# Experts and attention in one program, the first step reordered, the padding zeroed later, one-hot products a slot later

## What is computed

```python
xn = _layernorm(x)                                   # (4, 1024, 512): 4096 tokens of 512
# attention of xn, four batches of 1024 tokens, causal
x_norm = layernorm(xn) * gamma + beta
q, k, v = x_norm @ qkv[:, :512], x_norm @ qkv[:, 512:1024], x_norm @ qkv[:, 1024:]
s = softmax(causal(q @ k.T / sqrt(512))) @ v @ o_proj + xn
# mixture of eight experts of hidden width 352, two for each token, and two shared ones
gates = softmax(xn @ router_w.T); the two largest, divided by their sum
routed = sum over the two of gate * (silu(xn @ wg[e]) * (xn @ wu[e])) @ wd[e]
shared = (silu(xn @ sg) * (xn @ su)) @ sd            # width 704 = 2 x 352
out = x + s * silu(routed + shared)
```

## Time and profile before

| | us |
|---|---|
| median of three runs (lowest, highest) | 1158.92 (1158.82, 1160.46) |
| the profiled execution's own time | 1158.34 |
| its span, first to last instruction | 1156.6 |
| TensorE busy | 1132.1 (98%) |
| VectorE, ScalarE, GpSimd busy | 570.5, 473.5, 423.4 |
| mean granted clock of TensorE | 0.998 |

### The profile page before, as it was taken

One profiled execution on the slowest core, in us unless ns is written; L12 is line 12 of the kernel. 1 busy time (PEld: TensorE's weight loads), 2 busy tenths in 40 slices (PEclk: granted clock), 3 DMA queues, 4 the chain that ended last, 5 costly groups with the idle time before them and its releaser, 6 DMA issues. The chain is left out here.

```text
span 1156.6 us, 21228 instructions
## 1 busy us (share of the span) xinstructions
PE 1132.1 (98%) x6598; PEld 627.3 (54%) x6599; DVE 570.5 (49%) x1236; ACT 473.5 (41%) x859; POOL 423.4 (37%) x656
## 2 busy tenths in 40 slices
PE   8899999999999999999999999998999999999997
PEld 5555555555555555555555555554454444444454
DVE  6866667677468322211221122111377467467467
ACT  5544444444332223322332233224645545654643
POOL 1363333332200122222222222212764764764663
PEclk9999999999999999999999999999999999999999
DMA  9889999989633589989898878776767668766355
GB/s 288 232 190 219 232 233 236 202 220 231 158 71 77 117 170 209 207 198 209 193 203 191 185 173 182 179 169 163 152 163 186 157 160 184 166 161 182 114 150 126
DMA packets 365004, 209.31 MB, mean 181 GB/s; under 512 B 304309, under 2 KB 314817, under 8 KB 364937
## 3 DMA queue, kind: packets, MB, share of 16 engines
q1 hardware_dynamic: 354104, 172.76, 64.7%
q0 software_dynamic: 10800, 35.69, 12.2%
q10 hardware_dynamic: 32, 0.02, 0.0%
HBM read 89.44 MB, written 46.01 MB: 117 GB/s over the span
## 5 line engine op out<-in xcount | busy, mean ns | idle before, releaser
L708 PE MATMUL pair<-arena 128*128 (+2 forms) x3240 | 506.2, 313 | 0.2 <-issue 0.2
L708 PEld LDWEIGHTS pair<-arena 128*128 128x128 f16 x3240 | 316.1, 98 | 182.6 <-issue 0.9
L1629 DVE SCALAR_TENSOR_TENSOR arena<-pair,slot_unit,arena 128x352 f32<-128x352 f32 x71 | 41.4, 583 | 268.8 <-ACT arena L1519 220.3
L715 PE MATMUL bank<-arena 128*128 x639 | 149.3, 379 | 1.3 <-DMA arena<-arena 1.3
L1519 ACT ACTIVATE arena<-pair,slot_unit 128x352 f32<-128x352 f32 x71 | 39.4, 555 | 205.5 <-PE pair L708 172.1
L1238 POOL COPY arena<-token_of 128x1 uint32 (+1 forms) x71 | 13.0, 183 | 271.3 <-issue 103.3
L715 PEld LDWEIGHTS bank<-arena 128*128 128x128 f16 x639 | 62.5, 98 | 67.7 <-issue 1.8
L1910 PE MATMUL pair<-arena 128*128 128x512 f16 (+3 forms) x576 | 97.5, 326 | 0.6 <-ACT arena L1979 0.6
L1923 PE MATMUL bank<-arena 128*128 128x512 f16 x411 | 93.4, 379 | 0.0
L1240 POOL DMA_INDIRECT arena<-xn_rows,arena x71 | 71.4, 1005 | 55.7 <-POOL arena L1238 54.1
L1895 PE MATMUL bank<-arena 128*128 128x512 f16 x384 | 86.0, 379 | 1.6 <-PEq L1058 1.6
(11 more groups left out here) (205 smaller groups left out, 1356.4 us busy)
## 6 DMA issues: line engine op xcount, KB each, us to landing
slot_rows<-arena SPq DMA_DIRECT2D x71, 256.0 KB
arena<-in_L_attn_x_dram SPq DMA_DIRECT2D x64, 256.0 KB, 3.6
xn_rows<-arena SPq DMA_DIRECT2D x32, 260.0 KB, 2.5
shared_rows<-arena SPq DMA_DIRECT2D x32, 256.0 KB
arena<-shared_rows SPq DMA_DIRECT2D x32, 256.0 KB
out_dram<-arena SPq DMA_DIRECT2D x31, 256.0 KB, 2.8
arena<-in_L_ffn_wg_dram SPq DMA_DIRECT2D x32, 176.0 KB, 3.1
arena<-in_L_ffn_wu_dram SPq DMA_DIRECT2D x32, 176.0 KB, 3.4
```

The lines of the kernel that those rows point to most:

```text
L708: last = pe.matmul(bank[:, 0:width], xt[:, a, c, :], weights(c, b, col, width), start=(c == 0 and i == 0), stop=(c == KC - 1 and i == 2))
L715: last = pe.matmul(bank[:, :], ht[:, a, c, :], weights(c, b), start=(start and c == 0 and i == 0), stop=(stop and c == HC - 1 and i == 2))
L1629: v.scalar_tensor_tensor(sbuf[u], u_banks[u][:, 0:H], slot_unit[u][:, 1:2], sbuf[u], ALU.mult, ALU.mult).then_inc(slot_h_ready, 1)
```

## The change

It has four parts.

1. The second block is gone. The attention's programs become functions that are called at the end of each engine's list in the one block. TensorE's first projection (`first_project`) stands between the down products of the last two slot tiles, and the order of the first two PSUM banks is swapped so that it has a free one. In place of the barrier each engine waits for what it needs: SP and GpSimd for all slot rows to be stored (`slots_stored`), ScalarE for the last slot product, and three of the first batch's projections for copies out of their banks.
2. In SP's queue the stores of tiles 0 and 1 and the first load of `w_down` go behind the first turn of h; on ScalarE and VectorE the second unit's h in the first step goes ahead of tile 2's x and of three of the four splits.
3. GpSimd's memset of the padding goes from between tiles 3 and 4 to behind the last tile.
4. One-hot table 6 is made half a step earlier, and products 1 and 4 are multiplied half a step later.

```diff
@@ fold_programs, sync
                 turn_x16(sp, 1)
-                for t in range(2):
-                    store_x16(sp, t)
@@ routing, hot_products_in
                 elif at == 9:
                     one_hot(dve, 5)
-                elif at == 10:
                     one_hot(dve, 6)
+                elif at == 10:
                     one_hot(dve, 7)
...
-                return {7: (0, 1), 8: (2,), 9: (3, 4), 10: (5,), 11: (6, 7)}.get(at, ())
+                return {7: (0,), 8: (1, 2), 9: (3,), 10: (4, 5), 11: (6, 7)}.get(at, ())
@@ expert_stages, sync
                     for i in in_chunks(0)[:1]:
                         load_in(i)
-                    for s in range(NT):
+                    load_x(3)
+                    turn_h(0)
+                    for t in range(2):
+                        store_x16(sp, t)
+                    load_down(0)
+                    for i in [*in_chunks(0)[1:], *in_chunks(1)[:1]]:
+                        load_in(i)
+                    for s in range(1, NT):
...
                     for j in range(T - 3, T):
                         store_slot_y(j)
+                    attn_sync(sp)
@@ expert_stages, gpsimd
                     x_low(pool, 3)
-                    if HR < P:
-                        pool.wait_ge(shared_lo, len(splits))
-                        pool.memset(w_down[HR:P, :, HC - 1], 0.0).then_inc(down_padded, 1)
-                        pool.wait_ge(down_padded, 1)
...
                     put(pool.memset(segment[:, :, 0:1], 0.0))
+                    pool.wait_ge(consts, n[0])
+                    if HR < P:
+                        pool.wait_ge(shared_lo, len(splits))
+                        pool.memset(w_down[HR:P, :, HC - 1], 0.0).then_inc(down_padded, 1)
+                        pool.wait_ge(down_padded, 1)
@@ expert_stages, tensor
                     slot_down(T - 2, 1, (T - 2) // 2)
+                    first_project(pe)
                     slot_down(T - 1, 0, (T - 1) // 2)
+                    attn_tensor(pe)
@@ first_step, scalar
                         split_hi(act, IN_SPLITS)
-                        split_hi(act, IN_SPLITS + 1)
+                        h_high(1, 1)
                         for t in normal_in(0):
                             x_high(t)
-                        h_high(1, 1)
-                        split_hi(act, IN_SPLITS + 2)
-                        split_hi(act, IN_SPLITS + 3)
+                        for n in range(1, 4):
+                            split_hi(act, IN_SPLITS + n)
@@ first_step, vector
+                        hidden(1, 1)
                         for t in normal_in(0):
                             normalise(dve, t)
-                        hidden(1, 1)
                         split_lo(dve, IN_SPLITS)
-                        split_lo(dve, IN_SPLITS + 1)
                         h_low(1, 1)
-                        split_lo(dve, IN_SPLITS + 2)
-                        split_lo(dve, IN_SPLITS + 3)
+                        for n in range(1, 4):
+                            split_lo(dve, IN_SPLITS + n)
@@ stage4
-            proj_banks = banks[6], banks[7], banks[0], banks[1], banks[2], banks[3]
+            proj_banks = banks[7], banks[6], banks[0], banks[1], banks[2], banks[3]
...
+            def slots_stored(eng):
+                eng.wait_ge(slot_y_done, SLOT_TILES)
+                eng.wait_ge(slot_rows_stored[0], (SLOT_TILES + 1) // 2 * 16)
+                eng.wait_ge(slot_rows_stored[1], SLOT_TILES // 2 * 16)
...
-            with nc.Block() as block:
...
+                slots_stored(sp)
...
+            def gpsimd(pool):
+                slots_stored(pool)
                     pool.memset(causal, 0.0).then_inc(causal_zeroed, 1)
...
+            def project(pe, b, g_):
...
+                if b == 0 and g_ == 1:
+                    pe.wait_ge(slot_y_ready, SLOT_TILES - 1)
+                elif b == 0 and g_ == 2:
+                    pe.wait_ge(slot_h_ready, SLOT_TILES)
+                elif b == 0 and g_ == PG - 2:
+                    pe.wait_ge(slot_y_ready, SLOT_TILES)
...
+            def first_project(pe):
+                pe.wait_ge(fold_loaded, QT * 16)
+                project(pe, 0, 0)
...
+                act.wait_ge(slot_y_done, SLOT_TILES)
```

712 lines of the change are left out of this document (353 added, 359 removed).

## The result

The changed kernel takes 1151.79 us, the median of six runs (1149.63 to 1154.26), beside 1157.89 us for the kernel before; the ratio is 0.9942, 95% interval 0.9930 to 0.9955. Run again later beside the experiments it took 1154.46 us (five runs) against 1159.18, ratio 0.9963 (0.9949 to 0.9977). So it saves 4.7 to 6.1 us. The first median is the forecast of 1151.8 us, but partly because the kernel before was 1.03 us faster in this comparison than in the three runs that the forecast started from: the forecast gain of 7.1 us lies above both measured gains, inside the interval of the first (5.2 to 8.1) and outside that of the second (2.7 to 5.9). The profiled execution took 1151.93 us, with a span of 1150.2. Two executions were slow ones, 1323.11 us in run 10 and 6861.79 us of the kernel before beside run 12; they count in the medians shown and not in the ratios.

The account below looks back on a forecast made before the run. TensorE, busy 98% of the span, was taken as the bound; gains 3.24, 0.94 and 3.25 less a 0.3 loss took 7.1 from 1158.34, giving 1151.2, plus 0.58 for the median: 1151.8 us, range 1149.8 to 1156.0.

Parts of the forecast that it names:

- The seam: Between experts and attention: the first projection fills TensorE's waits, the second starts at 795.00 instead of 798.24; gain 3.24 us.
- Rival 3, the attention restarts late: First attention batch: later gathers delay ScalarE's exp and TensorE waits; up to 3.9 us lost, 1155.7 us; chance 8%.
- The one-hot products: Around 360 us: VectorE bounds the stage, its last table is ready 0.94 us earlier; gain 0.94, between 0 and 3.18.
- The padding: Moving GpSimd's 6.92 us memset from 58.70 removes TensorE's waits at 78.88, 96.76 and 103.46; gain 3.25, between 0 and 3.7.
- The first step: Expert half's start: wait at 48.88 grows to 3.1, that at 55.76 nearly goes; loss 0.3, between gain 1.9 and loss 2.6.
- The order of the two engines: First step: GpSimd's low part of x starts ahead of VectorE's weight split; if VectorE comes first, TensorE starts 1.6 us later.
- the sum itself: Over the whole kernel: the four terms added, -3.24 - 0.94 + 0.3 - 3.25 = -7.1 us.
- a microsecond won ahead of it stays won: Behind the seam TensorE does not wait until far into the last batch, so time won earlier is kept in full.
- The clock: First step: a fall to 1.2 GHz for 3.4 us after TensorE idles, costing 1.7 us; part of rival 1.
- rival 1: First step: the store lands slowest, costing 2.3 us delay and 1.7 us of lowered clock; 1155.8 us; chance 12%.
- Rival 2, the early waits belong to the DMA engines: Early expert steps: busy DMA engines keep most or all of the padding's gain away; 1153.7 or 1155.1 us; chance 15%.

Follow-up runs that it names:

- run 10: Changed kernel with the eighth one-hot product half a step later on TensorE, and VectorE's naming of the tokens with it; 1152.67 us, ratio 0.9938.
- run 12: The changed kernel as it is, profiled and timed a second time; 1154.46 us, ratio 0.9963 against the kernel before.
- run 4: Kernel before with the other three parts but no common program: experts and attention stay two programs with the barrier; 1156.28 us, ratio 0.9980.
- run 6: Kernel before with the new order of the first step alone; 1157.46 us, ratio 0.9996.
- run 9: Kernel of run 8 with the store and load of x in steps 1 to 3 behind the turn of h; 1156.45 us, ratio 0.9967.
- run 1: Changed kernel with the order of the first step undone, other three parts kept; 1151.02 us, ratio 0.9934.
- run 2: Changed kernel with GpSimd's zeroing of the padding put back in its old place; 1154.37 us, ratio 0.9958.
- run 7: Changed kernel with the first down product waiting for one piece of the down weights instead of two; 1154.16 us, ratio 0.9958.
- run 8: Kernel of run 7 with the second turn of h ahead of tile 2's turn, store and load in SyncE's queue; 1152.04 us, ratio 0.9939.
- run 5: Changed kernel with 18 matmuls that compute nothing put into TensorE's 3.03 us wait in the first step; 1157.13 us, ratio 0.9985.
- run 11: Changed kernel with the edits of run 7, run 8, run 9 and run 10 together; 1155.22 us, ratio 0.9967.

## Why the prediction was right or wrong

**The seam** was forecast at 3.24 and came to 3.19, with no gap between the last down products and the second projection. (Between the eighth product and the seam the seam's gain can be blurred: waits for DMA of 0.22 to 1.13 us stand in the slot tiles of six of the eleven profiles with one program and of none of the three with two.) *Rival 3, the attention restarts late,* came true at a part of its price. From the second projection to TensorE's last wait the three profiles with two programs take 347.54 (before), 348.11 (run 4) and 347.73 us (run 6); of those with one program the five without a new wait take 348.12 (run 10) to 348.51 us (run 12). That is about 0.6 more in the mean, though run 4 and run 10 are equal, with 0.3 of it in the last wait for DMA, 1.37 to 1.43 instead of 1.08 to 1.18. On top come new waits of TensorE near 830 or 1012 us: none in the three with two programs; 0.57, 0.21, 1.65, 1.58, 2.22 and 1.36 in six of the eleven others, 0.7 on average. How one arises is seen at the longest (run 9), beside the same place in run 1:

```profile
1010.61 0.72 ACT L2028 ACTIVATE arena<-arena,gate 128x512 f32<-128x512 f32 x1 [4.40 <-DMA arena<-slot_rows,arena]
1011.24 0.61 ACT L2035 ACTIVATE arena<-arena 128x512 f32<-128x512 f32 x1
1011.76 0.58 ACT L1998 ACTIVATE arena<-bank 128x512 f16<-128x512 f32 x1
```

```profile
1008.23 0.72 ACT L2013 ACTIVATE arena<-arena,gate 128x512 f32<-128x512 f32 x1 [2.25 <-DMA arena<-slot_rows,arena]
```

ScalarE waits for gathered rows, and a projection's copy (L1998) and the scores' exp stand behind that on its queue. This is the mechanism that the rival named, if further back than the first scores. Three of the six new waits are of this kind; the three near 830 us are for VectorE, and what held VectorE was not followed. That the seam brings any of them is not shown by an edit: six of eleven against none of three is little.

**The one-hot products** were forecast at 0.94, as one wait of about 2.4 and one of 0.3; they came as 2.26 and 0.15, and the terms give 0.93. VectorE as the bound of this stage was right, and run 10 shows that its lag can't be stepped over by TensorE alone.

**The padding** was forecast at 3.25. That it makes TensorE's waits go was right: alone it is 3.76. (The prediction names for VectorE's wait of 2.64 and ScalarE's of 4.89; they stand in the earlier trace rows.)

**The first step** was forecast as a loss of 0.3, with waits of 3.1 and nearly none and the second product at 55.8, which is 19.47 us behind the first unit. Run 4 shows the forecast as it was meant: a wait of 3.03 and almost none, the clock up, the product at 19.60, a loss of 0.17. The changed kernel's own profile has 3.03 and none, but with the fall of the clock the product is at 20.67, a loss of 1.24. The order of the two engines was forecast with GpSimd first, without which TensorE would start 1.6 later. In this profile it came so, GpSimd's low part 0.55 us ahead of VectorE's split:

```profile
47.91 1.16 POOL L291 TENSOR_TENSOR arena<-arena 128x512 f16<-128x512 f32 x1
```

```profile
48.46 2.89 DVE L238 SCALAR_TENSOR_TENSOR arena<-arena 128x1024 f16<-128x1024 f32 x3 [0.54 <-ACT arena L232]
```

GpSimd held VectorE about as forecast: the first of the three splits takes 1.70, 0.5 more than the 1.22 of the one at 46.03, and GpSimd's part ends 0.6 behind its start. So it ends at 50.16, against 50.8 in the forecast, in which GpSimd started 0.6 later. The Trainium skill, "SBUF — State Buffer", section "SBUF: two separate sides", has the later of the two block until the first is done; by that, as an estimate from these rows, the split would end at 49.07 + 1.22 = 50.29, and GpSimd's part in run 12 at 49.71 + 1.22 + 1.16 = 52.09. They end at 50.16 and 51.94, so the rows agree to 0.15 us. The other order, which the prediction feared, came in runs 2, 7, 10 and 12: with the first wait in place the second product is then at 20.41 to 20.82, 0.8 to 1.2 behind run 4, where 1.6 had been forecast. So the loss of 0.3 was the price of the good case alone. The other eight profiles with the new order of SyncE's queue lose 1.0 to 1.6 at the second product: by a fall of the clock, by VectorE ahead of GpSimd, or by a late transpose.

Two of the prediction's steps failed here. The first is the sum itself, which added the two parts as if they were independent. They work on the same waits: alone they are worth 3.76 and 2.26, together 3.38 to 4.15, and with the zeroing moved the order is worth -0.4 to 0.4. The forecast for both, 2.95, is near only because a term of the wrong sign was added to one for which the partner left less. The second is "a microsecond won ahead of it stays won". The reason given for it was that TensorE does not wait behind the seam, and there the 0.6 and 0.7 above came back. Ahead of the seam the sum used it too, without a reason: in the first seven steps the second product can be put 4.26 us earlier, and one step later a new wait takes 2.26 of it and a fall of the clock 1.7 (run 8).

**The clock** (the half of rival 1) did fall in the first step of the profiled execution, behind the 3.03 us in which TensorE had nothing. It cost 1.3 us in place. Against run 4, whose first step is the same to 0.01 us up to there, it cost 1.07 at the second product and 0.77 at the eighth one-hot product. Runs 5 and 12 keep the clock up and gain nothing, but each for its own reason: a transpose that landed after 5.16 us, and VectorE ahead of GpSimd. So the fall explains nearly all of the 1.24, and some 0.8 of it lasted. That is one pair of profiles; how much of a fall is covered on average stays open.

*Rival 2, the early waits belong to the DMA engines,* was given 15% and was partly right. The waits at 78.88, 96.76 and 103.46 did go. But once they had, each further gain in these steps ended in new waits, nearly all for DMA (runs 7 to 9 and 11).

Between the forecast gain of 7.1 and the measured 4.7 to 6.1 stand 1.3 that the attention gives back on average (0.6 and 0.7), against 0.4 to 1.2 more than told from the padding and the first step; the marks thus make 6.2 to 7.0. The lower end fits the first set. The rest, up to 2.3 us, is not explained; two sets of runs of one kernel differ by 1.4 us in their gains, and the kernel before has only one profile. That the first median hit the forecast is thus in part luck: the 1.3 of the attention was put at nothing, the early parts were worth more than told, and the kernel before ran 1.0 us faster than the median from which the forecast started. No run found a version that is faster than the changed kernel beyond doubt; the lowest medians are 1151.02 (run 1) and 1151.79.

## What to carry to other kernels

When two edits remove waits in the same stage, price the second against the kernel that has the first: find what each wait would be with the other gone, and take the larger, not the sum. Where TensorE is ahead of a stage whose DMA engines are full, an earlier start can turn into a longer wait one step later, so look at which resource is full in the steps behind, not only at the wait removed. And ahead of a comparison of two profiles, take a mark behind the part that varies by itself (here the opening, 3.8 us) and count from it. Profile the same program twice before a difference under 1 us is given a cause: here it is the second profile that shows two orders of two engines, which change a wait by 1.2 us.

## What was not expected of the hardware

**The same wait is followed by a fall of the clock in one profile and not in another.** Between the opening and TensorE's last matmul each fall stands at a wait of TensorE: it begins between 1.0 us before and 1.3 us behind the end of the wait. Of the 22 waits of 1.96 us or more there, 10 were followed by one, and none of the shorter ones; but a wait of 3.03 us was followed by a fall in three profiles and not in run 4, and the one of 2.25 or 2.26 at the products by one in two of nine. All were of 3.4 us at 0.50, or two of these in a row (run 7, at 4.36 us of wait). The Trainium skill, "TensorE: Matmul & The Clock Gate", section "Why this matters for your kernels", warns of idle gaps between bursts of matmuls; by these rows the warning holds for gaps as short as 2 us here, in 10 of 22 cases. How far an execution's time follows: over 92 runs of the changed kernel and eleven of its variants (against each kernel's own mean), 0.001 less of mean granted clock goes with 1.06 us more.

**The same transpose lands at different times.** In the nine profiles with the new order of SyncE's queue (all but the kernel before and runs 1, 8, 9 and 11) the second turn of h in the first step landed 3.31 to 5.16 us after its issue: 3.31 in the changed kernel, 4.23 in run 7, 5.16 in run 5. That spread of 1.85 is more than two of the four terms of the forecast.
